# A last stage laid out by expert units, its output product in a bank of its own, and its weights made a stage earlier

## The chip, the cores and the metric

One core of a Trainium2 chip runs the whole program once. The metric is device time in microseconds (us). TensorE (PE), VectorE (DVE), ScalarE (ACT), GpSimd (POOL) and SyncE (SP) each run their own instruction list and meet only at semaphores.

## What is computed

Two transformer-like layers over x of 8 batches x 512 rows x 128 features: attention, a top-2 mixture of experts, a selective scan, and a second mixture of experts. The change is in the last two. In the reference's words, cut:

```python
x = x + ga * L1_attn_ref(h, ...)          # the scan's output added, h = layernorm(x)*(1+ca)+sa
h = layernorm(x) * (1 + cb) + sb
xc = silu(pw_w @ causal_conv3(h) + pw_b); x1 = h + xc
rw = softmax over the top 2 of x1 @ router_w.T + router_b          # 8 experts
ye = silu(x1 @ expert_w + expert_b)       # all 8 experts, 128 -> 128 each
moe = (sum_e rw_e * ye_e) @ out_w.T + out_b
g = norm_w * rms_normalised(x1 + moe)
x = x + gb * (g + gelu(g @ ff_down_w.T + ff_down_b) @ ff_up_w.T + ff_up_b)
```

## The kernel before, in words

The program has five stages, `parts_0` to `parts_d`. After stages 1 to 3 each engine signals an end and waits for all others (`part`, L2503, `end_stage` and `meet`), so no engine is in the last stage, `ffn1` (L2064), before all have left the scan's, `ssm` (L1679). Every engine's order is written out by hand; `Signals` turns names into semaphore waits.

**Scan's stage.** `dve` (L1861) runs a chain of products on T(0)...T(10), [128, 512] each, with ACT giving Exp, Ln and Exp (L1850, L1852, L1854) between them. `low_weights` (L1915, L1918 and L1920) stands in that chain while ACT works. PE then makes eight output products into banks `YB` (L2045 to L2056), DVE adds each to X (L1992), and after the fourth takes the statistics of batch 0 (`dve_bn_group` 0, L1651). Pool turns these into the layer norm's factors (`pool_ln_group`, L1657).

**Last stage.** A batch is 4 tiles of 128 rows. The front of a batch: normalise (`z`, Pool L2121 and ACT L2177), transpose (`zt`, L2392), scale (`hidden`), split into a high and a low part (`hidden` L2195, `low` L2281), convolution product of nine matmuls (`pw`, L2397), `silu`, sum on Pool (`x1`, L2129), split again (`x1h`, `x1l`), router (`route` L2406, `logits`, `best`, `second`, `gates`). Then come the experts: unit u is one tile of 128 rows through all 8 experts (`expert`, L2414, eight matmuls of 512 columns in the bank pair 0-1 or 2-3), ACT's Silu into `ye` (L2219), and DVE's weighted sum `combine(p)` over the pair p of units 2p and 2p+1 (L2333 twice, L2336 fourteen times). Once a batch is summed: `ct` (transposes), `turned`, `out` (L2435, product and x1 added), `bn_out` on DVE (L2339), `rms` on Pool (L2103), `norm` on ACT (L2228, L2233), `hr` (transposes), `fd` (L2450), `gelu` (L2243), `fo` (L2456: per tile one product of the normed rows by DG, L2463, and one of the gelu by FUG, L2464), `final` on DVE (L2345) and the store.

The order of all engines runs over pairs p (L2470 on PE): `front` puts the front of batch p+1 into pair p (0 to 6), so that fronts end at half the experts. `misc` (L2380) deals banks 4 to 7 in turn to every product that is no expert's; a product waits until the one four before it has been read (for `out` that is ACT's `norm`). Pool makes GF, FUG and DG (`last_weights`, L2139: GF is L2163, FUG L2142 and L2146, DG L2150) during pairs 0 to 5, ahead of `rms`.

## Time and profile before

| what | us |
|---|---|
| median of 3 runs | 1002.78 |
| lowest, highest | 998.81, 1006.16 |
| the profiled execution | 1009.28 |
| its span, first to last instruction | 1007.5 |
| PE busy in the span | 840.4 (83%) |
| DVE, ACT, POOL busy | 738.3, 632.3, 496.3 |
| mean granted TensorE clock | 0.909 |

The span is 1.8 us shorter than the time of its own execution. The scan's stage starts near 740 us and ends near 820, the first expert's matmul is at 834.08, the last expert's Silu at 976.15, and the last add ends at 1005.02. A granted clock of 1.00 is 2.4 GHz, one of 0.50 is 1.2 GHz; a 512-column matmul then starts every 0.23 or 0.43 us.

### The profile page before, as it was taken

What the parts mean: (1) busy time and instruction counts of PE and PEld (TensorE: products, weight loads), DVE (VectorE), ACT (ScalarE), POOL (GpSimd) and SP (SyncE); (2) the same over time, 40 slices, a digit from 0 to 9 for tenths busy, and PEclk for the clock granted to TensorE, in tenths of its full rate; (3) what the DMA queues carried; (4) which work ended last, traced back from release to release, by engine and by line L of the source; (5) the groups of instructions that cost most, each with busy time, mean ns of one, the idle gap of its engine ahead of it and who ended that gap; (6) DMA issues with size and microseconds to landing.
All of it is one profiled execution on the core that took longest, in us unless ns stands there. A gap on an engine that the chain in (4) does not pass through costs nothing.

```text
span 1007.5 us, 14225 instructions
## 1 busy us (share of the span) xinstructions
PE 840.4 (83%) x4630; PEld 461.7 (46%) x4630; DVE 738.3 (73%) x1561; ACT 632.3 (63%) x1113; POOL 496.3 (49%) x794
## 2 busy tenths in 40 slices
PE   5689999999988988887796999889946559977986
PEld 4312222222212222221475877777733247766774
DVE  6687878788888778862485888858749577966771
ACT  2157777877766777676484777566715736545562
POOL 3715282727265666355552167656657046653211
PEclk9669999999999999898798999999967878978997
DMA  7735454545536264102115266556360000000000
GB/s 238 153 107 186 91 182 97 166 112 152 125 120 160 107 172 124 68 24 109 52 36 177 97 221 247 195 190 217 115 237 10 24 1 1 0 1 11 22 21 32
DMA packets 45477, 110.78 MB, mean 110 GB/s; under 512 B 7886, under 2 KB 20814, under 8 KB 40086
## 3 DMA queue, kind: packets, MB, share of 16 engines
q1 hardware_dynamic: 39260, 97.93, 32.5%
q0 software_dynamic: 4992, 10.36, 3.0%
q10 hardware_dynamic: 1152, 1.58, 0.5%
q8 instruction: 37, 0.61, 0.3%
q14 instruction: 36, 0.29, 0.1%
HBM read 57.65 MB, written 51.03 MB: 108 GB/s over the span
## 4 chain that ended last, share of the span: by engine, by line
PE 49%; DVE 19%; issue 10%; POOL 10%; ACT 8%; DMA 4%; SPq 0%; another core or an unknown queue 0%; POOLq 0%; DVEq 0%; ACTq 0%
PE PS L1083 10%; DVE mx L891 9%; PE PS L1072 6%; PE PS L1053 4%; PE PS L320 4%; PE PS L322 3%; PE PS L321 3%; POOL yd L1298 3%; DMA HT<-xs 2%; ACT E L798 2%; PE PS L1035 2%; PE PS L1020 1%; ACT ov L804 1%; PE PS L2425 1%; PE PS L2428 1%
## 5 line engine op out<-in xcount | busy, mean ns | idle before, releaser
L891 DVE TENSOR_REDUCE mx<-PS 128x2 f32<-128x1024 f32 x256 | 305.5, 1221 | 76.4 <-PE PS L1053 70.6
L798 ACT ACTIVATE E<-PS 128x512 f32<-128x512 f32 x512 | 277.0, 599 | 85.8 <-PE PS L1072 81.7
L1072 PE MATMUL PS<-Q,K 51*128 51x512 bf16 x512 | 166.0, 396 | 10.6 <-ACT E L798 6.9
L1053 PE MATMUL PS<-K,Q 48*128 48x512 bf16 x512 | 140.6, 409 | 27.1 <-DVE mx L891 26.7
L1083 PE MATMUL PS<-E,V 128*9 128x512 f32 x1024 | 140.1, 620 | 19.5 <-ACT ov L804 18.8
L1298 POOL DMA_INDIRECT yd<-yt,goes x92 | 94.6, 1028 | 49.2 <-DVE yt L1474 25.6
L1072 PEld LDWEIGHTS PS<-Q,K 51*128 51x128 bf16 x512 | 37.0, 95 | 162.1 <-ACT E L798 97.2
L1462 DVE TENSOR_TENSOR Gl<-Gf,Gh 128x512 fp32r<-128x512 f32 x117 | 82.2, 719 | 31.6 <-ACT Gh L1333 22.1
L513 POOL DMA_INDIRECT xs<-HT,pos x64 | 63.8, 996 | 79.5 <-ACT E L798 45.2
L1327 ACT ACTIVATE Gf<-PS,WR 128x512 f32<-128x512 f32 x92 | 63.1, 689 | 48.7 <-PE PS L322 39.3
L2336 DVE SCALAR_TENSOR_TENSOR cb<-ye,gt,cb 128x128 f32<-128x128 f32 x224 | 65.5, 366 | 0.0
L665 POOL CAST mh<-mx 128x32 bf16<-128x32 f32 x16 | 3.4, 211 | 113.1 <-DVE mx L891 113.1
L2219 ACT ACTIVATE ye<-PS 128x1024 f32<-128x1024 f32 x32 | 32.8, 1024 | 37.0 <-PE PS L2428 37.0
L1053 PEld LDWEIGHTS PS<-K,Q 48*128 48x128 bf16 x512 | 29.1, 95 | 58.0 <-DVE mx L891 49.6
L1083 PEld LDWEIGHTS PS<-E,V 128*9 128x9 f32 x1024 | 15.2, 88 | 65.5 <-issue 35.1
L1457 DVE CAST Gh<-Gf 128x512 fp32r<-128x512 f32 x62 | 29.4, 473 | 18.5 <-ACT Gf L1327 17.5
L320 PE MATMUL PS<-Hh,WR 128*128 128x512 f32 x92 | 41.0, 445 | 0.0
L1333 ACT ACTIVATE Gh<-Gf 128x512 fp32r<-128x512 f32 x62 | 39.2, 632 | 2.0
L321 PE MATMUL PS<-Gh,WR 128*128 128x512 f32 x92 | 36.9, 401 | 0.0
L320 PE MATMUL PS<-Gh,WR 128*128 128x512 f32 x92 | 36.8, 400 | 0.0
L322 PE MATMUL PS<-Hl,WR 128*128 128x512 f32 x92 | 36.8, 400 | 0.0
L321 PE MATMUL PS<-Hh,WR 128*128 128x512 f32 x92 | 36.8, 400 | 0.0
(420 smaller groups left out, 1895.1 us busy)
## 6 DMA issues: line engine op xcount, KB each, us to landing
WR<-wsd SPq DMA_DIRECT2D x23, 1028.0 KB
xs<-zero SPq DMA_DIRECT2D x8, 2112.0 KB, 7.4
wsd<-wsp SPq DMA_DIRECT2D x8, 1024.0 KB, 4.1
HT<-xs SPq DMA_DIRECT2D x23, 264.0 KB
dqk<-SPL SPq DMA_DIRECT2D x30, 192.0 KB, 2.8
Q<-dqk SPq DMA_DIRECT2D x14, 384.0 KB
K<-dqk SPq DMA_DIRECT2D x14, 384.0 KB
stage<-in_w SPq DMA_DIRECT2D x9, 516.0 KB
```

The source lines that it names most:

```text
L320: e.matmul(o, wh, xh, start=start, stop=False)
L321: e.matmul(o, wl, xh, start=False, stop=False)
L322: return e.matmul(o, wh, xl, start=False, stop=stop)
L513: e.indirect_dma_start(out=xs[:, :], out_offset=bass.IndirectOffsetOnAxis(ap=pos[:, x, i:i + 1], axis=0), in_=HT[:, i, :], in_offset=None) ...
L798: e.activation(E[:, m % 4, n % 4], PS[:, bank["exp", n], :], ACT.Exp).then_inc(*k.inc("exp", n))
L891: e.tensor_reduce(mx[:, 2 * s % 96:2 * s % 96 + 2], PS[:, o:o + 2, :], AX.X, ALU.max, negate=True).then_inc(*k.inc("max", s))
L1053: return e.matmul(PS[:, o + n % 2, :], Q[r, b % 3, h // 2, qt * P:(qt + 1) * P], K[r, b % 3, h // 2, :], start=True, stop=True)
L1072: e.matmul(PS[:, o, :], K[r, b % 3, h // 2, kt * P:(kt + 1) * P], Q[r, b % 3, h // 2, :], start=True, stop=True).then_inc(*k.inc("exp_mm", n))
L1083: p = e.matmul(PS[32 * j:32 * j + 9, PVB, :], V[:, b % 3, kt, 4 * g + j, :], E[:, m % 4, j, :], start=(kt == 0), stop=(kt == 3))
L1298: e.indirect_dma_start(out=yd[:, :], out_offset=bass.IndirectOffsetOnAxis(ap=goes[:, n % 8, t:t + 1], axis=0), in_=yt[:, n % 2, t * P:(t + ...
L1462: e.tensor_tensor(Gl[:, u % 8], Gf[:, u % 3], Gh[:, u % 8].bitcast(F32), ALU.subtract).then_inc(*k.inc("gl", u))
L2336: m = e.scalar_tensor_tensor(o, y, g, o, ALU.mult, ALU.add)
```

## The change

The end of the scan's stage is no longer a meeting of the engines, and both stages count as one for the semaphores. Pool makes FUG, GF and a new GN (the norm's weight times the gate, per batch) in the scan's stage, after its last `power`; DG goes, and with it PE's product by DG. In its place Pool multiplies the normed rows by GN and adds them to X (`gated`). ACT loads one table set by name before Exp, makes the experts' high part earlier, and touches Silu at the stage's end. DVE makes EWl in the scan's stage, adds batch 0's four tiles on their own with their statistics, then the rest; in the last stage it does `low(0)` before the next statistics, which come in three groups, and x1 of batch 0. PE, ACT and the steps of a batch are ordered by units u with a lag each (`due`). The output product has bank 7 (the last batch's has bank 0) and waits for the `norm` of the batch before; all others share banks 4 to 6, batch 0's first three products use banks 0 to 2. `ct` is due at lag 7, ahead of the `hr` of the batch before; `gelu` precedes the Silu of its unit. On Pool `rms` comes before the same pair's `x1`.

```diff
--- before.py
+++ after.py
...
-        LNG = {0: (0, 4), 1: (4, 12), 2: (12, NT)}
+        LNG = {0: (0, 4), 1: (4, 12), 2: (12, 20), 3: (20, NT)}
...
+                def last_weights():
+
+                    each = lambda n: W[n].unsqueeze(1).to_broadcast([P, 8, P])
+                    k.wait_ge("p3")
+                    k.wait_ge("gb1")
+                    e.tensor_scalar(W["fuT"], W["fuT"], 0.25, None, ALU.mult).then_inc(*k.inc("p"))
+                    e.tensor_tensor(GN[:], GB1[:], each("nwB"), ALU.mult).then_inc(*k.inc("gn"))
+                    k.wait_own("p")
+                    e.tensor_tensor(FUG[:], GB1[:], each("fuT"), ALU.mult).then_inc(*k.inc("fug"))
+                    k.wait_ge("bg1h")
+                    k.wait_ge("bg1l")
+                    e.tensor_tensor(GF, GB1[:], each("fubB"), ALU.mult).then_inc(*k.inc("gf"))
...
                 power(5)
+                last_weights()
                 pool_ln_group(e, k, 0)
...
                 next_weights(4)
+                next_weights(0)
                 out_weights()
+                e.preload_act_table_set("natural_log_exp_and_others")
                 k.wait_ge("zabs")
...
-                next_weights(0)
                 next_weights(2)
                 next_weights(3)
                 k.wait_ge("scan")
                 e.activation(Th[:], T(10), ACT.Copy).then_inc(*k.inc("ch"))
+                e.activation(scr[:, 3:4], half[:, 0:1], ACT.Silu)
...
-                    e.tensor_scalar(cl[:, 0:8], mf[:, 1, 5, :], W["nw"], None, ALU.mult).then_inc(*k.inc("gbn"))
...
+                    k.wait_ge("ewh")
+                    e.tensor_tensor(EWl, W["ewT"], EWh.bitcast(F32), ALU.subtract).then_inc(*k.inc("ewl"))
...
+                for t in range(4):
+                    k.wait_ge("y_mm", t)
+                    e.tensor_tensor(X[:, t, :], X[:, t, :], PS[:, YB[t], 0:P], ALU.add).then_inc(*k.inc("y0"))
+                    k.wait_own("y0")
+                    m = e.bn_stats(stats[:, t, :], X[:, t, :])
+                m.then_inc(*k.inc("bn", "g", 0))
                 for j, (hf, t) in enumerate(YJ):
-                    xv = X[:, 16 * hf + t:16 * hf + 16:4, :]
+                    a = 0 if hf else 1
+                    xv = X[:, 16 * hf + 4 * a + t:16 * hf + 16:4, :]
                     k.wait_ge("y_mm", j)
...
-                    if j == 3:
-                        k.wait_own("ys")
-                        dve_bn_group(e, k, 0)
...
-            DG = stage[:].rearrange("p a n -> p (a n)")[:, 0:1024].rearrange("p (b n) -> p b n", b=8)
...
+            FIRST = {"zd": 0, "pw": 1, "r1": 2}
+            UNITS = 4 * NB
+
+            def due(u, lag):
+
+                b = (u - lag) // 4
+                return (u - lag) % 4 == 0 and 0 <= b < NB, b
...
+                def gated(b):
+
+                    k.wait_ge("hs", b)
+                    k.wait_own("gn")
+                    if b:
+                        k.wait_own("xn")
+                    e.tensor_tensor(hg[:], hs[:, b % 2], GN[:, b:b + 1, :].to_broadcast([P, 4, P]), ALU.mult).then_inc(
+                        *k.inc("hg", b))
+                    k.wait_own("hg")
+                    e.tensor_tensor(xtiles(b), xtiles(b), hg[:], ALU.add).then_inc(*k.inc("xn", b))
 
                 e.memset(Hd[:, :, 0:2], 0.0).then_inc(*k.inc("const", "hd0"))
                 z(0)
                 pool_ln_group(e, k, 1)
                 z(1)
-                x1(0)
-                pool_ln_group(e, k, 2)
-                for p in range(NP + 6):
+                k.wait_own("gf")
+                for p in range(NP + 4):
                     if p + 1 in front:
                         z(front[p + 1])
...
+                        pool_ln_group(e, k, 2)
+                    if p == NP + 2:
+                        rms(NB - 1)
+                    if p % 2 == 0 and 0 <= p // 2 - 3 < NB:
+                        gated(p // 2 - 3)
+                    if p % 2 == 0 and 0 <= p // 2 - 2 < NB - 1:
+                        rms(p // 2 - 2)
                     if p in front:
                         x1(front[p])
...
-                    if 2 <= p < 6:
-                        last_weights(p - 2)
-                    if p % 2 == 0 and 0 <= p // 2 - 2 < NB:
-                        rms(p // 2 - 2)
+                    if p == 2:
+                        pool_ln_group(e, k, 3)
                     if p % 2 and p // 2 < NB:
                         shift(p // 2)
+                gated(NB - 1)
...
                 z(0)
-                e.activation(scr[:, 3:4], half[:, 0:1], ACT.Silu)
                 hidden(0)
                 z(1)
                 silu(0)
                 x1h(0)
...
+                for u in range(UNITS + 10):
+                    p = u // 2
+                    if u % 2 == 0 and p in front:
                         hidden(front[p])
...
+                    for lag, step in ((7, turned), (11, norm), (12, hr), (13, gelu)):
+                        now, b = due(u, lag)
+                        if now:
+                            step(b)
+                    if u < UNITS:
+                        expert(u)
...
                     k.wait_ge("fo_mm", b)
-                    k.wait_ge("xg", b)
+                    k.wait_ge("xn", b)
...
+                k.wait_own("ys")
+                low(0)
                 dve_bn_group(e, k, 1)
-                k.wait_ge("ewh")
-                e.tensor_tensor(EWl, W["ewT"], EWh.bitcast(F32), ALU.subtract).then_inc(*k.inc("ewl"))
-                low(0)
-                dve_bn_group(e, k, 2)
+                k.wait_ge("sx", 0)
+                e.tensor_tensor(X1[:, 0], sx[:, 0], Hd[:, 0, 2:514], ALU.add).then_inc(*k.inc("x1f"))
                 x1l(0)
                 logits(0)
                 best(0)
                 second(0)
-                for p in range(NP + 6):
+                dve_bn_group(e, k, 2)
+                for p in range(NP + 7):
+                    if p % 2 == 0 and 0 <= p // 2 - 4 < NB:
+                        final(p // 2 - 4)
...
+                    if p == 0:
+                        dve_bn_group(e, k, 3)
...
-                    if p % 2 and 0 <= p // 2 - 3 < NB:
-                        final(p // 2 - 3)
...
                 def misc(what, b, *free):
-                    if len(uses) >= 4:
-                        k.wait_ge(*uses[-4])
-                    bank[what, b] = 4 + len(uses) % 4
+                    if b == 0 and what in FIRST:
+                        bank[what, b] = FIRST[what]
+                        return bank[what, b]
+                    if len(uses) >= 3:
+                        k.wait_ge(*uses[-3])
+                    bank[what, b] = 4 + len(uses) % 3
...
                     k.wait_ge("cT", b)
-                    bk = misc("out", b, "hs", b)
+                    if 0 < b < NB - 1:
+                        k.wait_ge("hs", b - 1)
+                    bk = bank["out", b] = 7 if b < NB - 1 else 0
...
-                        e.matmul(o, hT[:, b % 2, t * P:(t + 1) * P], DG[:, b], start=True, stop=False)
-                        m = e.matmul(o, ff[:, b % 2, t * P:(t + 1) * P], FUG[:, b], start=False, stop=True)
+                        m = e.matmul(o, ff[:, b % 2, t * P:(t + 1) * P], FUG[:, b], start=True, stop=True)
...
-                for p in range(NP + 6):
-                    if p in front:
+                for u in range(UNITS + 12):
+                    p = u // 2
+                    if u % 2 == 0 and p in front:
                         zt(front[p])
...
+                    for lag, step in ((8, out), (12, hr), (13, fd), (15, fo), (7, ct)):
+                        now, b = due(u, lag)
+                        if now:
+                            step(b)
+                    if u < UNITS:
+                        expert(u)
+                    if u % 2 == 0 and p - 1 in front:
                         route(front[p - 1])
...
+                    if u % 2 and p in front:
                         pw(front[p])
...
-            if 1 <= st <= 3:
+            if 1 <= st <= 2:
                 end_stage(e, k, st, LAST[i])
                 meet(e, k, st)
...
-            book.stage = max(st, 1)
+            book.stage = min(max(st, 1), 3)
```

## Rows read from the trace of the kernel before

**Rows 1.** Busy time in stretches: expert stage in three parts, one batch, two holes.
```profile
core 0: us, PE busy (x) PEld busy (x) DVE busy (x) ACT busy (x) POOL busy (x), PEclk, DMA share, GB/s
834.08:903.24 69.16, 63.05 (x298) 50.46 (x297) 55.31 (x179) 38.24 (x62) 40.91 (x43) 0.87 0.00 1
903.24:976.15 72.91, 62.09 (x343) 51.56 (x342) 52.40 (x184) 44.22 (x63) 22.26 (x46) 0.95 0.04 15
976.15:1005.02 28.87, 19.95 (x108) 15.56 (x106) 7.92 (x27) 9.32 (x18) 4.73 (x16) 0.83 0.07 28
943.26:957.74 14.48, 13.22 (x76) 10.91 (x76) 10.74 (x38) 9.37 (x14) 3.64 (x9) 1.00 0.05 19
882.67:893.22 10.55, 6.87 (x22) 5.10 (x21) 4.22 (x15) 4.02 (x9) 4.72 (x12) 0.51 0.01 2
904.87:916.88 12.01, 6.24 (x29) 5.54 (x28) 3.81 (x13) 5.21 (x9) 6.74 (x10) 0.72 0.00 1
```

**Rows 2.** Timeline of the two holes (start, length, engine, line, idle before and its releaser).
```profile
879.73 3.32 POOL L2150 TENSOR_SCALAR stage<-p,cl 128x128 f32<-128x128 f32 x4
...
886.52 1.14 ACT L2233 ACTIVATE hs<-PS,lnw 128x128 f32<-128x128 f32 x4 [6.20 <-POOL lnw L2119]
...
887.81 0.77 PE L320 MATMUL PS<-Hdh,PWh 128*128 128x512 f32 x1 [3.68 <-ACT hs L2233]
...
908.10 1.06 PE L2410 MATMUL PS<-p,X 128*128 128x8 f32 x8 [2.83 <-POOL X L2131]
...
912.10 0.77 PE L2463 MATMUL PS<-stage,hT 128*128 128x128 f32 x2 [2.94 <-ACT hs L2233]
```

**Rows 3.** Timeline, one output product in the steady part: its start, the next expert's.
```profile
943.26 0.49 PE L2463 MATMUL PS<-stage,hT 128*128 128x128 f32 x2 [1.26 <-ACT ff L2247]
...
945.06 0.48 PE L2425 MATMUL PS<-rwp,ones 128*128 128x512 f32 x1
```

**Rows 4.** Timeline of VectorE and GpSimd where they meet.
```profile
860.38 2.39 POOL L2142 TENSOR_TENSOR FUG<-GB,p 128x1024 f32<-128x1024 f32 x1
...
860.55 2.27 DVE L2316 TENSOR_TENSOR wk<-wk 128x32 f32<-128x32 f32 x1
...
903.17 3.76 DVE L2336 SCALAR_TENSOR_TENSOR cb<-ye,gt,cb 128x128 f32<-128x128 f32 x14
...
904.20 3.84 POOL L2131 TENSOR_TENSOR X<-sx,Hd 128x512 f32<-128x512 f32 x1 [6.41 <-ACT sx L2202]
...
927.15 4.76 DVE L2336 SCALAR_TENSOR_TENSOR cb<-ye,gt,cb 128x128 f32<-128x128 f32 x14
...
928.38 1.29 POOL L2136 TENSOR_TENSOR X<-X,GA 128x512 f32<-128x512 f32 x1
```

**Rows 5.** Timeline of the scan's chain.
```profile
800.49 1.28 ACT L1852 ACT_TABLE_LOAD   x1
...
800.97 1.22 DVE L1920 TENSOR_TENSOR BGp<-GA,BGp 64x1024 fp32r<-64x1024 f32 x1
...
802.45 0.69 DVE L1966 SCALAR_TENSOR_TENSOR tb<-tb 128x512 f32<-128x512 f32 x1 [0.25 <-ACT tb L1852]
```

**Rows 6.** Timeline of the entry into the last stage.
```profile
820.82 1.65 DVE L1654 BATCH_NORM_STATS2 stats<-X 128x6 f32<-128x128 f32 x8 [0.65 <-POOL scr L2500]
...
821.75 1.28 ACT L2250 ACT_TABLE_LOAD   x1
...
827.77 0.88 ACT L315 ACTIVATE Zd<-X,lnw 128x128 f32<-128x128 f32 x2 [3.20 <-POOL lnw L1677]
...
829.69 0.69 ACT L2202 ACTIVATE sx<-PS,cl 128x512 f32<-128x512 f32 x1 [1.04 <-PE PS L322]
```

**Rows 7.** Timeline of the tail, after the last expert.
```profile
977.61 3.76 DVE L2336 SCALAR_TENSOR_TENSOR cb<-ye,gt,cb 128x128 f32<-128x128 f32 x14
...
986.73 0.60 PE L2389 MATMUL PS<-p,cb 128*128 128x128 f32 x4
...
1000.51 0.80 PE L2463 MATMUL PS<-stage,hT 128*128 128x128 f32 x2 [0.78 <-ACT ff L2247]
...
1004.33 0.69 DVE L2348 TENSOR_TENSOR X<-PS,X 128x512 f32<-128x512 f32 x1 [7.98 <-PE PS L2464]
```

More of the change, by code:

```diff
@@ L1635, in adaln_kernel @@
         GF = GA1[:]
+        FUG = sb("FUG", [P, 8, P])
+        GN = sb("GN", [P, 8, P])
         EWh, EWl = wsp[:, 0:1024], wsp[:, 1024:2048]
@@ L2254, in act @@
                 x1h(0)
[L2255 to L2256 removed]
+                for u in range(UNITS + 10):
+                    p = u // 2
+                    if u % 2 == 0 and p in front:
                         hidden(front[p])
[L2258 to L2278 removed]
+                    for lag, step in ((7, turned), (11, norm), (12, hr), (13, gelu)):
[4 more added lines that the diff above has]
+                        expert(u)
+                    if u % 2 == 0:
+                        if p in CHOICE:
+                            tanh(CHOICE[p])
+                        if p + 1 in front:
+                            z(front[p + 1])
+                        if p - 1 in front:
+                            x1h(front[p - 1])
+                    elif p in front:
+                        silu(front[p])
             def dve(e, k):
@@ L2579 @@
         "owT": I["L1_ffn_out_w"].T, "nw": col(I["L1_ffn_norm_w"]), "fdT": I["L1_ffn_ff_down_w"].T, "fdb": col(np.tile(I["L1_ffn_ff_down_b"], 4)),
-        "fuT": np.tile(I["L1_ffn_ff_up_w"].T, (4, 1)), "fubB": rows(I["L1_ffn_ff_up_b"]),
+        "fuT": np.tile(I["L1_ffn_ff_up_w"].T, (4, 1)), "fubB": rows(I["L1_ffn_ff_up_b"]), "nwB": rows(I["L1_ffn_norm_w"]),
     }
```

84 lines of the change are left out of this document (18 added, 66 removed).

## The prediction

> **What bounds the kernel now.** I read the busy time by stretches first, then the waits, then the timeline around each long one. The change touches only what lies behind 780 us, so I cut that into parts [rows 1]. From the first expert matmul (834.08) to the start of unit 14 (903.24), while fronts run, PE is busy 63.1 of 69.2 us at a clock of 0.87. From there to the last Silu (976.15) it is busy 62.1 of 72.9 at 0.95. The tail takes 28.9 us with PE busy 20.0. PE is the bound of the first two, with holes; the tail is a chain.
>
> In a steady batch of 14.48 us PE works 13.22 and DVE 10.74 [rows 1]; PE's whole idle is 1.26 us ahead of `fo`, which waits for the gelu [rows 3]. So PE bounds it, but DVE is only 2.5 us behind.
>
> Two holes stand out. At 882.67 to 893.22 PE works 6.87 of 10.55 us, at half clock; at 904.87 to 916.88 it works 6.24 of 12.01 at 0.72 [rows 1]. The reader is to see what stands before each [rows 2]: Pool makes half of DG for 3.32 us just when `bn_out(0)` is done, so `rms(0)` is late, ACT stands 6.20 us in front of `norm(0)`, and PE waits 3.68 us with a convolution product whose bank is still `out(0)`'s. In the second, `route(7)` waits 2.83 us for x1 on Pool, and `fo(0)` 2.94 us for the bank that `norm(1)` reads, since `rms(1)` stood behind that x1.
>
> **The change part by part** (sum against the profiled execution: span 1007.5, time 1009.28).
>
> *1. Scan's chain, +2.2.* Three table loads of 1.28 us stand in it [rows 5]. One set for both functions lets Ln follow Exp at once, but DVE's L1966 then waits for DVE itself: L1920 ends at 802.19, L1966 started at 802.45 [rows 5]. So −0.25. On the other side Pool now makes GN and FUG during the last fronts of the scan, 2.39 us each by the same product of 1024 columns [rows 4], and can hold up DVE's `low(5)`, `low(6)` there: 0 to 1.5 us, I take 0.4. GF waits for `bg1l`, that is for L1920, and so starts in the middle of DVE's chain. The nearest row is FUG at 860.38: a DVE instruction with two inputs that began behind it took 2.27 us in place of some 0.2 [rows 4]. Between L1966 and L1968 DVE has a gap for its own semaphore, into which a waiting Pool product can step. 0 to 2.4 us; I take 2.05. EWl moves into DVE's idle time before the transposed inputs land (1.2 us, hidden). Bounds of the part: −0.7 to +3.9.
>
> ScalarE: Activation LUTs of the Trainium skill, section on table sets, says that the set named in the change holds exp and ln both; if it did not, the loads would stay and the −0.25 would be a +1. No row of before can show it.
>
> *2. Entry, +0.3.* The common end (0.65 us from it to the first work) and the Silu load of 1.28 [rows 6] go, and batch 0's statistics come some 1.0 us earlier since four adds of one tile replace one of four tiles. `hidden(0)` started when the load had ended, 823.03; without load, and with all before it 1.1 earlier, it starts at about 821.5. But DVE's statistics of batches 1 and 2 (1.65 us) now stand behind `low(0)`, so their factors come at about 829.4 instead of 827.7, and ACT's order puts `z(1)` (0.88) in front of `silu(0)`: silu starts at 830.4, before at 829.69 [rows 6]. x1 on DVE (0.69 as L1966, against 1.1 on Pool) gives back 0.4. What is late next is `z(1)`. Net +0.3; bounds −2.5 and +1.5.
>
> *3. First stretch (69.2 us), −8.0.* The first hole goes: DG is no longer made here, `rms(0)` follows its statistics, and no convolution product waits for `out`'s bank. That is 3.68 idle plus half of 6.87 busy at 0.51, 3.4, together 7.1 [rows 1, 2]. GF, FUG's two steps and the other half of DG (four blocks of 2.4 to 3.3 us on Pool, by [rows 2, 4]) stop blocking DVE: 1 to 4, I take 1.9. Against it, about 1.0: the statistics of 20 tiles at 0.2 each (1.65 for eight [rows 6]) now stand between DVE's other steps, and the first `gated` comes, on a DVE that is busy 55.3 of 69.2. Bounds −3 to −12: PE's work at full clock is 63.05 less about 6 for the slow part, so 57 is the floor.
>
> *4. Second stretch (72.9 us), −12.8.* Second hole: 5.77 idle and 2.4 by the clock (6.2 busy at 0.72, of which the slow part is from 910 on), 8.2 in all; x1(7) can still be late, so I count 6.5. DG's product: a `fo` takes 1.80 us for eight pairs [rows 3], half of them go: 0.90 × 5 = 4.5. The wait for gelu: 1.26 × 4 = 5.0, since the gelu now stands ahead of its unit's Silu and `fo` comes two experts later. Against it, the two products of `gated` per batch. PE would need 13.22 − 0.90 = 12.32 us a batch. DVE has 10.74, and two more Pool products of 1.1 to 1.3 us (the one at 928.38 [rows 4]) that read SBUF: up to 12.9 to 13.3. I take a period of 13.0, so 0.7 × 4.5 batches = 3.2 back. −6.5 − 4.5 − 5.0 + 3.2 = −12.8. Bounds −16 (nothing held up) and −6.
>
> How long the two hold each other up is the open price. SBUF — State Buffer of the Trainium skill, "Who interferes with whom", says that the first to start has the shared pair for one whole instruction and the other blocks. By that rule a Pool product waits at most one DVE instruction, then takes 1.0 from DVE. The row at 927.15 agrees (the burst grew from 3.76 to 4.76 while `shift` took 1.29), the row at 904.20 doesn't: that Pool sum took 3.84 us, and ended 1.1 us behind a burst that lost nothing [rows 4]. By the page alone the period would be 13.3, by the second row 12.3.
>
> *5. Banks.* A ring of three in place of four: each product waits for one released three uses ago, which are ACT copies or DVE's `logits` and are long done by then. Nothing; if DVE lags by more than 3 us, `fd` waits for `final`, within the bounds above. `out` waits for the `norm` before it: from there to the next `norm` lie out 2.0, combine 4.2, statistics 0.9, rms 2.8, norm 1.1, that is 11 to 12 us in a period of 13. Hidden, with about 1 to spare.
>
> *6. Tail (28.9 us), −7.2.* `combine(15)` ends at 981.37; `ct(7)` waits behind `hr(6)` until 986.73 [rows 7]: 5.4 go. PE is still at full clock then, where now `out(7)` runs at the slow one: −1.7. The last `fo` takes 3.8 us (1000.51 to 1004.33 [rows 7]) and loses half: −1.9. `norm(7)` will stand behind `gelu(6)` on ACT: +0.8. `gated(5)` meets `combine(15)`: +1.0. Sum −7.2; bounds −4 and −10. `gated(7)` (2.4) lies beside hr, fd, gelu, fo (over 5).
>
> Sum: 2.2 + 0.3 − 8.0 − 12.8 − 7.2 = −25.5. The span becomes 982.0, its execution 983.8. This execution was 6.5 above the median of its runs, so I forecast 977.3.
>
> **Rivals.**
> *A. The port pair binds DVE.* DVE's 10.74 plus three Pool products in full, plus lags: 14.1 us a batch, +5 in the second stretch, and +5 in the first, where DVE is busiest. For it: 2.27 us lost to one product. Against: bursts that lost nothing. −15.5: 987.
> *B. PE binds alone.* No lock in the scan (−2.0), period 12.3 (−3.2), first stretch near its floor (−3): −33.7, 969.
> *C. Slower.* The `gated` pair waits for a burst of 3.84 us each, as x1 did, and `rms` of the next batch stands behind it on Pool: 7.7 less the 2.4 of the products = 5.3 late, so `norm`, the single bank of `out`, and PE wait, and the clock falls as in the first hole, 2.8 more. 8.1 for each of six batches: +48.6 on the forecast, 1026. It decides once each batch loses over 4.2 us. Against it: `gated(b)` is released about 7 us before `rms(b+1)` has its statistics.
> *D. It does not do what it says.* The holes move rather than close (ACT's order in pairs 6 and 7, x1 behind `rms`): only fo, the gelu wait and half the tail count, less the scan's loss: −4.5 − 5.0 − 3.6 + 3.2 + 2.5 = −7.4, 995.
>
> **How the numbers follow.** Forecast 0.52, its own range 970 to 984; A 0.22; B 0.14; D 0.08; C 0.04. The range of 963 to 991 takes in A and B with their bounds and leaves out D and C and a little of each edge. A measurement of this kernel tells about 1% (10 us) from no change: faster by more is forecast, A and B, 0.90 with a small part of D; within 1% most of D, 0.06; slower 0.04.
>
> **What would show it.** Right: the stretch of 32 units shortens from 142 to about 121; a steady batch takes about 13.0 us with no PE wait ahead of the FUG products; DVE's burst often reads 4.8 rather than 3.8; no Pool weight work behind the first expert; `ct(7)` directly after the last combine; a DVE instruction of over 2 us in the scan's chain beside Pool's GF; one table load there. Wrong: a batch near 14.5, an ACT wait for Pool's rms of over 3 us in every batch, or PE's clock at 0.5 more than once between the first and the last expert.

## The result, and the profile after

The changed kernel takes 991.77 us (median of 8 runs, 990.16 to 996.03), the kernel before beside it 999.19 (8 runs). The ratio is 0.9922, with an interval of 0.9901 to 0.9943: 7.8 us gained by the ratio, 7.4 between the medians, where the forecast had 25.5. The kernel is faster, but by under 1%, the outcome to which I had given 0.06. 991.8 lies just outside my range of 963 to 991, and nearest to the 995 of rival D.

The profiled run of the changed kernel took 990.16, its span is 988.3. First the stretches, cut as before: first expert to unit 14, then on to the steady part, three batches of it, and the rest (the windows of the kernel after; columns as in [rows 1]).

```profile
core 0: us, PE busy (x) PEld busy (x) DVE busy (x) ACT busy (x) POOL busy (x), PEclk, DMA share, GB/s
828.49:893.24 64.75, 59.57 (x298) 48.70 (x297) 55.63 (x193) 41.16 (x65) 31.81 (x49) 0.95 0.01 1
893.24:914.65 21.41, 18.23 (x97) 15.30 (x96) 19.74 (x64) 11.71 (x18) 10.43 (x20) 0.92 0.04 13
914.65:954.86 40.21, 36.37 (x194) 28.98 (x193) 38.38 (x113) 28.00 (x40) 17.54 (x28) 1.00 0.06 21
954.86:988.30 33.44, 18.11 (x98) 13.22 (x96) 15.20 (x43) 11.40 (x23) 16.01 (x30) 0.86 0.08 31
```

Beside [rows 1]: the first stretch fell from 69.16 to 64.75. PE is no longer the busiest in the steady part: DVE works 38.38 of 40.21, PE 36.37. The batches there are of two kinds in turn. Counted from `bn_out` to `bn_out` they take 12.8 and 14.6 us, in both profiles of this kernel, so two batches take 27.4 and one 13.7 in the mean, where a batch took 14.48. The window of 40.21 holds two short ones and one long. A long one has these two waits in it (PE's `out`, then DVE's weighted sum):

```profile
931.63 0.47 PE L2477 MATMUL PS<-rwp,ones 128*128 128x512 f32 x1 [1.28 <-ACT hs L2264]
...
941.62 0.48 DVE L2358 TENSOR_SCALAR cb<-ye,gt 128x128 f32<-128x128 f32 x2 [1.79 <-ACT ye L2249]
```

The stages, set side by side (us; "scan" is from DVE's first step behind the last transposed input to the copy of the scan's result; "end" is from the start of the last `final` to the span's end). A second profile of each kernel stands beside the first:

```
                      before   before 2   after   after 2   forecast   got, 1st pair   2nd pair
up to the scan chain   798.6     789.1    791.5     793.0        0         -7.1          +3.9
scan                    10.8      10.8     12.5      12.5     +2.2         +1.8          +1.8
entry                   24.7      23.8     24.5      24.9     +0.3         -0.2          +1.0
first expert to u. 14   69.2      67.4     64.8      65.1     -8.0         -4.4          -2.3
unit 14 to last Silu    72.9      72.9     65.5      65.4    -12.8         -7.4          -7.5
last Silu to final      28.2      28.5     22.1      22.0     -7.2         -6.1          -6.5
end                      3.2       3.1      7.5       7.6        0         +4.3          +4.4
```

From the scan chain to the end the first pair of profiles reads 208.9 and 196.8, that is -12.1, and the second 206.5 and 197.4, that is -9.1, against -25.5. The second is nearer to what the medians say. What lies ahead of the scan chain differs by 9.5 us between two executions of the kernel before. Only its last piece belongs to the change: from the issue of the load of `p` to the landing of the last transposed input it is 54.2 us in both profiles of before and 54.9 in both of after. So the part that I called the scan's costs 1.8 and another 0.7, beside my 2.2. No run shows what the 0.7 is.

By the first pair 13.4 us are missing. What they are made of is visible in four places. Two are in the list of PE's waits (behind 820 us of the kernel after; engine, line, what it waited for: total, times, longest):

```profile
engine line waited for: us in total, times, longest us
PE PS L2443 <- POOL X L2163: 5.9, 3, 3.2
PE PS L2443 <- DVE X L2379: 4.0, 1, 4.0
PE PS L2477 <- ACT hs L2264: 3.1, 4, 1.3
PE PS L2493 <- DVE X L2373: 2.8, 3, 1.0
PE PS L2501 <- ACT ff L2278: 2.4, 3, 0.8
PE PS L2420 <- DVE lg L2319: 2.3, 1, 2.3
...
```

L2477 is the first matmul of `out`: it waits for `norm`, since `out` has one bank. L2493 is `fd`, which waits for `final` through the ring of three. Part 5 of the prediction had both at nothing. L2443 is `route`, waiting for Pool's x1. L2420 is `zt`, whose bank of the ring DVE's `logits` had still to read, and part 5 had those "long done by then".

The third place is DVE (its timeline in the steady part, then Pool's):

```profile
922.51 3.75 DVE L2361 SCALAR_TENSOR_TENSOR cb<-ye,gt,cb 128x128 f32<-128x128 f32 x14
926.20 0.87 DVE L2367 BATCH_NORM_STATS2 stats<-PS 128x6 f32<-128x128 f32 x4
...
927.48 6.88 DVE L2361 SCALAR_TENSOR_TENSOR cb<-ye,gt,cb 128x128 f32<-128x128 f32 x14
```

```profile
930.29 1.29 POOL L2168 TENSOR_TENSOR X<-X,GA 128x512 f32<-128x512 f32 x1
931.57 1.30 POOL L2177 TENSOR_TENSOR hg<-hs,GN 128x512 f32<-128x512 f32 x1
932.94 1.27 POOL L2180 TENSOR_TENSOR X<-X,hg 128x512 f32<-128x512 f32 x1
```

`shift` (the sum of X and GA on Pool, L2168) and both products of `gated` run back to back in one burst of combines, and that burst takes 6.88 in place of 3.75: 1.04 for each product. [rows 4] had 1.0 for one. The other burst of the batch loses nothing.

The fourth is the end (Pool's last instruction, then DVE's):

```profile
979.23 1.27 POOL L2180 TENSOR_TENSOR X<-X,hg 128x512 f32<-128x512 f32 x1
```

```profile
980.83 0.69 DVE L2373 TENSOR_TENSOR X<-PS,X 128x512 f32<-128x512 f32 x1 [2.30 <-PE PS L2501]
```

Pool ends at 980.50, the last add starts at 980.83, and the span ends at 988.3. In the kernel before the end comes 3.2 behind the start of that add, and in this one 7.5. The timeline has nothing between. But the view of source line L135, at which the kernel closes, has what each engine's sequencer does there: a DRAIN, with its length in ns and its start in us (the kernel after, then before):

```profile
L135 POOLq DRAIN  x1: 8918/8918/8918, 979.2 to 979.2; - x1
...
L135 DVEq DRAIN  x1: 728/728/728, 980.8 to 980.8; - x1
```

```profile
L135 POOLq DRAIN  x1: 8688/8688/8688, 994.5 to 994.5; - x1
...
L135 DVEq DRAIN  x1: 730/730/730, 1004.3 to 1004.3; - x1
```

Pool's DRAIN runs to 988.1, that is 7.6 us past Pool's last instruction, and the span ends 0.2 later. In the kernel before it also ends 7.6 past Pool's last instruction (995.6), at 1003.2, but that is ahead of the last add and costs nothing.

### The profile page after: what moved, and what is told of

It reads as the page before. It is cut to its first block, busy times and chain, and to the rows that moved or that the text cites. A ratio compares the mean times of both kernels' runs of the same rounds, so it can differ in the third digit from the quotient of the medians.

```text
span 988.3 us, 14132 instructions
## 1 busy us (share of the span) xinstructions
PE 826.2 (84%) x4566; PEld 446.7 (45%) x4566; DVE 756.5 (77%) x1564; ACT 631.0 (64%) x1110; POOL 507.2 (51%) x811
## 4 chain that ended last, share of the span: by engine, by line
PE 38%; DVE 24%; POOL 16%; issue 11%; ACT 7%; DMA 2%; SPq 0%; POOLq 0%; DVEq 0%; ACTq 0%
PE PS L1083 12%; POOL yd L1298 9%; DVE mx L891 8%; PE PS L1072 7%; PE PS L1053 5%; DVE cb L2361 4%; ACT E L798 2%; PE PS L1035 2%; ACT ov L804 1%; PE PS L1020 1%; PE PS L320 1%; PE PS L322 1%; PE PS L321 1%; POOL Gl L1290 1%; PE PS L1040 1%
## 5 line engine op out<-in xcount | busy, mean ns | idle before, releaser
L1298 POOL DMA_INDIRECT yd<-yt,goes x92 | 95.0, 1032 | 44.4 <-issue 22.9
L1462 DVE TENSOR_TENSOR Gl<-Gf,Gh 128x512 fp32r<-128x512 f32 x117 | 86.0, 749 | 22.4 <-ACT Gh L1333 19.1
L1327 ACT ACTIVATE Gf<-PS,WR 128x512 f32<-128x512 f32 x92 | 63.4, 689 | 39.5 <-PE PS L322 38.7
L2361 DVE SCALAR_TENSOR_TENSOR cb<-ye,gt,cb 128x128 f32<-128x128 f32 x224 | 76.0, 412 | 0.0
L2249 ACT ACTIVATE ye<-PS 128x1024 f32<-128x1024 f32 x32 | 32.6, 1026 | 18.0 <-PE PS L2465 14.5
L322 PE MATMUL PS<-Gl,WR 128*128 128x512 f32 x92 | 36.3, 395 | 0.0
L320 PE MATMUL PS<-Gh,WR 128*128 128x512 f32 x92 | 36.3, 394 | 0.0
```

Of the source, the lines that this page charges most:

```text
L320: e.matmul(o, wh, xh, start=start, stop=False)
L322: return e.matmul(o, wh, xl, start=False, stop=stop)
L1298: e.indirect_dma_start(out=yd[:, :], out_offset=bass.IndirectOffsetOnAxis(ap=goes[:, n % 8, t:t + 1], axis=0), in_=yt[:, n % 2, t * P:(t + ...
L1327: e.activation(Gf[:, u % 3], PS[:, u % 3, :], ACT.Gelu_apprx_tanh, bias=w[:, fc:fc + 1]).then_inc(*k.inc("gelu", u))
L1462: e.tensor_tensor(Gl[:, u % 8], Gf[:, u % 3], Gh[:, u % 8].bitcast(F32), ALU.subtract).then_inc(*k.inc("gl", u))
L2361: m = e.scalar_tensor_tensor(o, y, g, o, ALU.mult, ALU.add)
```

## The experiments

Each ratio is to the kernel before, with its interval; "base" is the changed kernel unless said. The five groups of runs, c to g, were compared on one chip each. A stage's length is read from one execution, which need not be a typical one: those of c3 (985.45) and d3 (991.78) were the longest of their runs.

**The same kernel again, and what `gated` costs.**

> The changed kernel unchanged, so that the others have a second profile of it beside them. Its profile had two parts that may be chance: it entered the scan's stage 7.8 us earlier than the kernel before, and 6.4 us lay between its last store's issue and the span's end, against 2.1 before. If both are chance of one execution, this one shows other numbers there and the same 249 us from the scan's first load to the last add. If they belong to the change, they come back. Median 991 to 993.

992.57, 0.992 [0.9887, 0.9953]; span 990.4, all stages from the scan chain on within 0.4 of the first profile, the end 7.6 again. So the 4.3 us of the end belong to the kernel.

```diff
-                    if p % 2 == 0 and 0 <= p // 2 - 3 < NB:
-                        gated(p // 2 - 3)
...
-                gated(NB - 1)
```

> Leaves out the normed rows times GN and their addition to X (gated), so the output lacks that term; nothing takes its place on PE. Theory 1, the port pair: gated's two Pool products lengthen one combine in every batch by about 2.1 to 2.6 us and DVE bounds the steady part; without them a batch falls from 13.7 to about 12.4 us and the whole by 6 to 10 us, to 982 to 986. Theory 2, the layout (bank 7 alone for the output, three banks for the rest, the order by units) costs what the forecast missed: the batch stays above 13.3 us, the whole falls by under 3 us.

This kernel leaves `normed rows x GN` and its addition to X out. 980.32, 0.9808 [0.974, 0.9877]. The end is 3.1, the tail 21.1, the 32 units take 123.5 (base 130.2), and every steady batch takes 12.5 (base 12.8 and 14.6 in turn). Theory 1 holds, with a total below its range of 982 to 986: it left out the end.

```diff
+                    for b in range(NB):
+                        m = e.tensor_scalar(GN[:, b], ident, cl[:, b:b + 1], None, ALU.mult)
...
+                        e.matmul(o, hT[:, b % 2, t * P:(t + 1) * P], GN[:, b], start=True, stop=False)
+                        m = e.matmul(o, ff[:, b % 2, t * P:(t + 1) * P], FUG[:, b], start=False, stop=True)
```

> The changed kernel with the normed rows' product back on PE (a diagonal weight per batch, made by Pool in the scan's stage), and gated gone from Pool. Theory 1: PE then bounds a batch at 13.2 us with DVE at 11, against 13.7 now: 2 to 4 us faster than the changed kernel, 988 to 990. Theory 2: PE gets 0.9 us a batch more and nothing comes back: 4 to 7 us slower than the changed kernel.

981.79, 0.9792 [0.9743, 0.9841]. The product that the change took from PE, back on PE, with its weight made in the scan's stage: 10 us better than on Pool (187.8 from the scan chain to the end, base 196.8). Its windows from unit 14 on (second line the steady part):

```profile
897.80:915.00 17.20, 16.33 (x93) 13.36 (x92) 16.35 (x56) 10.22 (x17) 4.47 (x8) 1.00 0.04 16
915.00:958.60 43.60, 43.60 (x255) 36.36 (x253) 35.62 (x122) 31.98 (x46) 14.67 (x34) 1.00 0.05 19
```

PE is busy in every moment of the steady part, 13.1 a batch. The 0.9 us that `gated` saved on PE is less than it cost: with `gated`, DVE has two stalls of 1.04 more a batch, the Silus of units 14 and 15 lie 9.1 us apart in place of 6.1, and Pool ends late. The gain is more than either theory had.

**The scan's lock.**

```diff
                     k.wait_ge("bg1l")
+                    k.wait_ge("rwp")
                     e.tensor_tensor(GF, GB1[:], each("fubB"), ALU.mult).then_inc(*k.inc("gf"))
```

> GF, Pool's product of 1024 columns, waits until DVE has left the scan's chain. The theory that its hold on the port pair stretched the chain's second step from 0.49 to 2.47 us: the chain from the landing of TP to Th shortens by 2.0 us and the whole by 1.5 to 2.0, to about 990. The rival, that it only moves the wait to Pool's own layer norm chain of batch 0, which follows GF on Pool: the chain shortens and the first expert starts at the same time, 0.

991.17, 0.9904 [0.9872, 0.9937]. The stage shows what the total can't: 10.5 in place of 12.5. The two lines, base (Pool, then DVE):

```profile
795.23 2.80 POOL L1749 TENSOR_TENSOR GA<-GB,p 128x1024 f32<-128x1024 f32 x1 [14.21 <-DVE BGp L1938]
```

```profile
795.12 0.69 DVE L1985 SCALAR_TENSOR_TENSOR tb<-tb 128x512 f32<-128x512 f32 x1
795.85 2.47 DVE L1987 TENSOR_SCALAR tb<-tb,cv 128x512 f32<-128x512 f32 x1
```

and the same DVE instruction of c4, beside which Pool waits:

```profile
797.36 0.49 DVE L1988 TENSOR_SCALAR tb<-tb,cv 128x512 f32<-128x512 f32 x1
```

So 1.98 us for one Pool product. Behind it the entry took 25.6 (base 24.5 and 24.9) and the units 132.1 (base 130.2 and 130.5), and the two us were gone again. Whether they must be is not shown: the last section has how much these stages differ by chance.

**The baseline, Pool's end, the entry, and a first combination.**

> The kernel before, unchanged, for a second profile. Its first profiled execution was 10 us over the median of its runs. If that excess was chance of the stages that the change does not touch, this one lands TP near 790 instead of 798.6, with the same 208.9 us from there to the end of the span; if it was in the last two stages, that stretch is some 4 us shorter here.

999.62, 0.9996 [0.998, 1.0012]; the stages stand in the table above. It is some of both: of the 11.9 us between the two executions 9.5 lie ahead of the scan chain and 2.4 in the last two stages.

```diff
                 def final(b):
+                    if b >= NB - 2:
+                        gated_v(b)
                     k.wait_ge("fo_mm", b)
```

> The changed kernel with the last two batches' gated products on DVE, which is idle in the tail, so that Pool's last work is the rms of batch 7. Between the last add on DVE and the span's end lay 6.8 us in both profiles of the changed kernel, but 2.4 to 2.5 in the kernels whose Pool ended earlier; each time the span ended 7.8 us after Pool's last instruction. Theory: a Pool that works late ends the program 7.8 us later, and that was on the path; now Pool ends some 5 us earlier and the store ends it: 3.5 to 4.5 us faster than the changed kernel, near 988. Rival: the end's length has another cause: no change.

989.04, 0.9894 [0.987, 0.9919]. Pool ends early, the end is 3.2 again, and 2.3 of the 4.3 come back ahead of `final`, where DVE now does two batches of `gated` in the chain. The interval meets the base's, so the total alone doesn't show a gain.

```diff
-                low(0)
                 dve_bn_group(e, k, 1)
+                low(0)
```

> The changed kernel with the statistics of batches 1 and 2 back ahead of low(0) on DVE. Theory: z(1) on ACT stood in front of silu(0) and came late since its factors did; now they are ready 3 us earlier and silu starts when the convolution's product ends: 24.6 us from Th to the first expert become 22.0 to 22.5, the whole 1.5 to 2.5 us faster. Rival: the half clock of PE bounds the way in, and low(0) becomes late: 0.

987.74, 0.9874 [0.9855, 0.9894]. The entry falls from 24.5 to 22.9; the units grow from 130.2 to 133.6 in the profile. The shorter entry is more than chance: it is 21.1 to 23.3 in the five profiles with this order and 24.3 to 25.6 in the eleven that have the old one and no common end. The timed gain of 4 us is larger than the entry's 1.6 and I can't place the rest.

d4 takes c3's product on PE, this order, and a tile of its own for GF, so that it needn't wait for the scan.

> Three repairs together: the normed rows' product on PE, statistics ahead of low(0), and GF in a tile of its own, made before DVE's scan chain. By the single runs: 10.8 us (diagonal product on PE) + 2.0 (GF out of the chain) + 2.3 (entry) under the changed kernel's 992: 976 to 979. If the gains overlap, 980 to 982.

977.73, 0.9764 [0.9742, 0.9786]: 14 us under the changed kernel, 23 under the one before. That lies in the 976 to 979 that were summed from the single runs.

**The bank of `out`.**

```diff
-                    if 0 < b < NB - 1:
-                        k.wait_ge("hs", b - 1)
-                    bk = bank["out", b] = 7 if b < NB - 1 else 0
+                    bk = own("out", b, "hs", b) if b < NB - 1 else 0
```

(`own` gives `out` banks 7 and 6 by turns from batch 3 on, `fo` bank 5, the others bank 4.)

> Base: the changed kernel. From batch 3 on the output product alternates between two PSUM banks, fo has one for itself, and ct, hr and fd share one, so that neither a product of the next batch waits for norm (PE stood 3.1 us in four waits for ACT's hs there) nor fd for final (2.8 us in three). Theory B1 (the single bank closes the loop: out waits for norm, norm for rms, rms for statistics that stand behind the long burst): the steady batch falls from 13.7 to 13.0 to 13.2, the floor that DVE's own busy time of 12.8 leaves, and the second stretch from 65.5 to 62 to 63.5. Theory B2 (DVE with three Pool products in it is the bound, and PE's waits are only its slack): the waits vanish from PE's list and come back as waits for ye's buffers or for cb; the batch stays at 13.6 to 13.7 and the time within 0.5 us.

994.04, 0.9918 [0.9886, 0.9949]. The steady batch (windows of e1, one batch each):

```profile
915.80:928.64 12.84, 12.51 (x69) 10.12 (x68) 12.82 (x38) 9.25 (x14) 4.90 (x6) 1.00 0.05 20
928.64:941.43 12.79, 12.50 (x69) 10.18 (x68) 12.77 (x38) 9.24 (x14) 6.62 (x12) 1.00 0.06 22
```

From batch 4 on every batch takes 12.8, in place of 12.8 and 14.6 in turn (13.7 in the mean), and DVE is busy in all of it: PE's wait for `norm` had been real, and DVE with three Pool products in it binds at 12.8. Theory B1 holds for the batch, by 0.9 us. From unit 15's Silu to the last one it is 52.5, where seven profiles with the base's banks and order there have 54.3 to 54.4. The total didn't move. Some of that is chance: the Silus of units 14 and 15, ahead of what this edit reaches, lie 10.2 us apart in place of 9.1, as PE is at half clock there behind the same wait of 3.2. And the tail is 1.1 longer, with a wait of 2.2 us for `cb` ahead of `ct(7)` (base 0.9).

```diff
+                    if p % 2 == 0 and 3 < p // 2 <= NB:
+                        k.wait_ge("comb", p - 2)
+                        shift(p // 2 - 1)
```

> Base: the changed kernel. From batch 3 on Pool's shift waits for the end of the combine burst in which gated runs, and so falls into the next, short one: bursts of about 5.9 and 4.8 us in place of 6.9 and 3.75. The sum of what DVE loses is the same. B2 (the sum binds): batch stays at 13.6 to 13.7. B1 (the long burst binds, since statistics and rms stand behind it and out's bank waits for them): the batch falls by up to 1 us, to 12.9 to 13.3, about 3 us in all. If a Pool product that comes to a running burst from idle waits for its end, as x1 did, shift loses up to 3.8 us on Pool, the statistics' rms behind it is late, and the batch gets longer than 13.7.

993.5, 0.9898 [0.9859, 0.9937]. The bursts became 5.8 and 3.8, with the third stall in the TENSOR_SCALAR ahead of the long one (0.74 and 0.89 for 0.48). Two batches took 12.5 and 14.0, a mean of 13.3 (base 13.7). From unit 14's Silu to the last it is 63.4 in both, but here 10.7 of it lie between units 14 and 15, ahead of the edit (base 9.1); from unit 15 on it is 52.7, base 54.3. So where in the batch the stalls fall does matter, as B1 had it, by 0.4 us a batch; the total can't show that. In the batch of 14.0 one `gated` product came to a running burst and took 2.81 us for 1.3.

**Pool's end, tested by itself.**

```diff
+                k.wait_ge("ff", NB - 1)
+                e.memset(hg[:, 0, 0:1], 0.0)
```

> Base: the fastest kernel so far (c3's product on PE, batches' statistics ahead of low(0), GF in its own tile; 977.73, last add to end 3.1 us). One memset of one column is added to Pool at its end, behind the last gelu, on a tile that nothing reads. Theory P (the program ends 7.8 us behind Pool's last instruction where nothing else is later): last add to end grows from 3.1 to 6 to 7, the time by 3 to 4 us. Rival (the 4.4 us came from gated itself, from its traffic or from the store of its batch): no change, 977 to 978.

984.56, 0.9811 [0.9763, 0.9859]; span 982.4. The median grew by 6.8, but the intervals of the two kernels meet, and the profile's entry is 2.2 longer by chance (last section); the end shows what the total can't. Pool's last instruction, and the start of the last add:

```profile
974.48 0.10 POOL L2205 MEMSET hg<- 128x1 f32 x1 [5.28 <-ACT ff L2278]
```

```profile
976.56 0.69 DVE L2373 TENSOR_TENSOR X<-PS,X 128x512 f32<-128x512 f32 x1 [4.39 <-PE PS L2503]
```

A memset of 0.10 us that nobody reads ends at 974.58, and the span ends 7.8 us later, as in the changed kernel (980.50 to 988.3). The end grew from 3.1 to 5.8. Theory P holds: a Pool instruction that has nothing to do with `gated` does the same, by the DRAIN behind it, which ends at 982.2.

**The common end.**

```diff
-            if 1 <= st <= 2:
+            if 1 <= st <= 3:
                 end_stage(e, k, st, LAST[i])
```

> Base: the changed kernel, with the common end of all engines behind the scan's stage put back and everything else left. My theory: the common end itself was worth little, since the first work of the last stage hangs on the scan's last product and its statistics either way. Entry 24.5 grows to 25 to 26.5, the time by 0.5 to 2 us. Rival (the common end was a main part of the gain, as engines could run ahead): +3 us or more, entry over 27.5.

996.88, 0.9939 [0.9909, 0.9969]. The entry is 26.3, 1.4 to 1.8 over the base's two profiles and 0.7 over the longest of the eleven with the base's order; the units took 3.2 more in the profile. The total's interval overlaps the base's. So what the common end cost lies between nothing and some 5 us, and I can't narrow that.

**Pool's queue at unit 14.** In the base x1(7) stands behind `rms(1)` (Pool's timeline; the Silu that makes sx(7) ends at 894.2):

```profile
893.64 0.57 POOL L2140 TENSOR_TENSOR lnw<-stats 128x4 f32<-128x4 f32 x1 [4.45 <-DVE stats L2367]
...
897.10 1.28 POOL L2163 TENSOR_TENSOR X<-sx,Hd 128x512 f32<-128x512 f32 x1
```

```diff
+                    if p == 6:
+                        x1(front[p])
                     if p % 2 == 0 and 0 <= p // 2 - 2 < NB - 1:
                         rms(p // 2 - 2)
```

> Base: the changed kernel. In pair 6 Pool's x1(7) comes ahead of rms(1), which waits 4.45 us for its statistics there while sx(7) is ready 2.9 us before x1 starts. Theory Q (Pool's queue order, not the lock, made the 3.2 us wait of route(7) and the half clock behind it, which is the largest single piece of what the second stretch missed): x1(7) starts at its Silu's end, the wait falls under 1 us, units 14 to 15 come 5.5 to 7 us apart in place of 9.1, and the stretch from unit 14 to the last shortens by 2 to 3. Rival (what is saved comes back, since norm(1), now 1.3 us later behind x1, holds out(2) and the combines): route's wait goes and the stretch stays within 0.5 of 65.5.

993.56, 0.9917 [0.9889, 0.9944]. Units 14 and 15 come 4.7 us apart in place of 9.1; 1.8 of the 4.4 are left at the last Silu (61.6 from unit 14's Silu to it, base 63.4), the rest came back as waits for `norm` at `out` (5.7 in four, base 3.1). The span didn't get shorter, since Pool sets its end: Pool's last instruction ends at 980.44 (base 980.50), as the first expert came 0.5 later and Pool's end lies 22.7 behind the last Silu (base 21.8), and the span ends at 988.3 in both. In this profile PE ran at half clock to the end, which put the last add at 984.30 in place of 980.83 and cost nothing: the end shrank from 7.5 to 4.0 (the last `fd` and `fo` of f1, then of the base):

```profile
979.34 2.07 PE L2495 MATMUL PS<-hT,fdn 128*128 128x512 f32 x2 [0.69 <-ACT hT L2274]
982.19 2.08 PE L2503 MATMUL PS<-FUG,ff 128*128 128x128 f32 x8 [0.78 <-ACT ff L2280]
```

```profile
977.73 1.13 PE L2493 MATMUL PS<-hT,fdn 128*128 128x512 f32 x2 [0.69 <-ACT hT L2272]
979.64 1.16 PE L2501 MATMUL PS<-FUG,ff 128*128 128x128 f32 x8 [0.78 <-ACT ff L2278]
```

> Base: f1, with the two banks for out of e1. If the 0.6 us per batch that e1 gave in the steady part is real and was only given back at the passage into it (PE's wait of 2.2 us for cb behind the late x1(7)), both gains stand here: 61 to 63 for the second stretch, 3 to 4 us under the changed kernel. If the gain of either is lost to the other's wait, 64 to 65.5 as before.

991.35, 0.9888 [0.986, 0.9915]. From unit 14's Silu to the last 60.5, base 63.4, f1 61.6: the batches, 14.0 and 13.0 in turn in f1, end up at 12.8. Both gains stand side by side. The wait of 2.2 us that I named stands in e1's tail, though, not at the passage, and here there is one of 2.8 in the tail. In the total the two edits are 3 us at most, inside the intervals.

> Base: the fastest kernel so far (d4), with x1(7) ahead of rms(1). There route(7) waits only 0.9 us, so I expect 0 to 1 us less: 976 to 978, a ratio to the kernel before of 0.975 to 0.977. Rival: rms(1) is later by x1's 1.3 and nothing is gained.

978.42, 0.9758 [0.9733, 0.9784]: the same as d4.

**The first stretch.**

```diff
+                    if p == 2:
+                        pool_ln_group(e, k, 3)
...
                     if p in front:
                         x1(front[p])
-                    if p == 2:
-                        pool_ln_group(e, k, 3)
```

> Base: the changed kernel. The factors of the last 12 tiles (Pool, 5.5 us with a pow of 2.30) come ahead of x1(3), where Pool stands idle 4.66 us, in place of behind it, where ACT's next normalisation waits 5.35 us for them, PE 2.33 us behind that, and the clock is halved for the 3.6 us after. Theory R (this one wait with its clock is what the first stretch missed of its 8.0): the wait for lg goes or falls under 0.5, the stretch from first expert to unit 14 falls from 64.7 to 60.5 to 62. Rival (x1(3), now up to 1.3 us later, takes the wait over, or the next front waits as long): the stretch stays within 1 us of 64.7.

995.86, 0.9927 [0.9903, 0.9952]. In the base ACT and PE stand like this:

```profile
860.00 0.88 ACT L315 ACTIVATE Zd<-X,lnw 128x128 f32<-128x128 f32 x2 [5.35 <-POOL lnw L1679]
```

```profile
862.37 0.79 PE L2420 MATMUL PS<-p,Zd 128*128 128x128 f32 x4 [2.33 <-DVE lg L2319]
```

In g1 both waits are gone, and unit 10's Silu comes 2.4 us earlier, counted from the first. Then:

```profile
876.19 1.88 PE L2443 MATMUL PS<-p,X 128*128 128x8 f32 x8 [3.19 <-POOL X L2163]
```

The next x1 is 3.2 us late, PE falls to half clock behind it, and unit 14 comes 65.2 behind the first Silu, base 63.1. The rival holds. The trace also says why this x1 is late: the Silu that makes its input ends at 871.42, but Pool stands with `rms(0)`, which is ahead of it in the same pair (Pool's timeline of g1):

```profile
871.28 0.58 POOL L2140 TENSOR_TENSOR lnw<-stats 128x4 f32<-128x4 f32 x1 [5.49 <-DVE stats L2367]
...
875.02 1.11 POOL L2163 TENSOR_TENSOR X<-sx,Hd 128x512 f32<-128x512 f32 x1
```

That is the queue of f1 once more, two pairs earlier. f1 turned the two in pair 6 alone; no run turns them in pair 4.

> Base: f3 (gated products on PE, statistics ahead of low(0), GF in its own tile, x1(7) ahead of rms(1)), with the same move of the factors. By theory R 3 to 4 us less than f3: 974 to 975.5, a ratio to the kernel before of 0.970 to 0.973. By the rival 977 to 979.

976.97, 0.975 [0.9714, 0.9787]. d4, f3 and g2 can't be told apart: 977 to 978.4, 23 to 25 us under the kernel before. Nor does g2 show more than f3 by its stages: unit 14 comes 65.0 behind the first Silu, in f3 63.4.

## Why the prediction was wrong

The direction and most mechanisms were right, the size wasn't: 7.8 for 25.5. The steps, in the prediction's order (two measured values are those of the first and the second pair of profiles):

*1. Scan, +2.2:* measured +1.8 in the chain and +0.7 ahead of it. Right in mechanism: one table load stands there, and DVE's L1987 took 2.47 beside GF. c4 shows that the whole of the 1.8 is that product.

*2. Entry, +0.3:* measured -0.2 and +1.0. `z(1)` in front of `silu(0)` is what is late; d3 gives 1.6 back by the order that I had named as the cause.

*3. First stretch, -8.0:* measured -4.4 and -2.3. The first hole closed, as foreseen. What failed is the sum "3.68 idle plus half of 6.87": it took both as gone for good. The stretch is a chain of fronts over four engines, and with the hole gone other waits of it decide: 2.33 us behind Pool's factors with half clock behind (862.8 to 866), 1.7 for x1. The 2.33 ends when DVE's `logits` free a bank, but these stand behind ACT's `x1h`, and that behind the normalisation that waits for the factors. g1 removed this wait, and the next took its place. So the floor of this stretch isn't PE's 57; in every kernel run, with `gated` or without, 63.1 to 65.2 us lie between the Silus of unit 0 and unit 14 (before: 69.6 and 68.4). What sets that floor I haven't settled; x1 behind `rms(0)` in pair 4 is the wait that stands next, and it is untested.

*4. Second stretch, -12.8:* measured -7.4 and -7.5. Two terms failed. First, "I count 6.5" for the second hole: x1(7) was late again, by more than before (3.2 us for 2.8 [rows 2]), since it still stood behind `rms(1)`. f1 shows it. Second, the period: 13.0 forecast, 13.7 measured, and 12.8 once `out` has two banks (e1). At 4.5 batches, as I had counted them, the 0.7 are 3.2 of the 5.4 us missing here, an estimate. My DVE sum, 10.74 plus two Pool products, was right to 0.1: it is the 12.8 of e1. The price of the lock was right too: 3.1 us for three products. "SBUF — State Buffer" of the Trainium skill, in "Who interferes with whom", says that the first to start holds the shared pair for one whole instruction. The products of 1.27 us cost DVE 1.04 each and the one of 2.80 cost 1.98, so trace and page agree there. For Pool's own wait they don't: an x1 that comes from idle at 852.09 takes 2.39 us, and ends 1.5 behind the burst that it met. Which of the two a product meets isn't settled.

*5. Banks, nothing:* wrong. "Hidden, with about 1 to spare" was computed with 4.2 for the combine between two norms. With the lock in it that burst is 6.9, so the spare 1 was gone by my own part 4; I didn't put the two together. `out` waited up to 1.29 a time, `fd` up to 1.0 for `final`. With both undone the batch lost 0.9.

*6. Tail, -7.2:* measured -6.1 and -6.5, right.

*The missing term.* "`gated(7)` lies beside hr, fd, gelu, fo" is true and hid the real cost: that Pool was still at work then. It is 4.3 us. The trace of before had it: Pool's DRAIN of 8.7 us at the kernel's close. Pool was done so early there that it cost nothing, and I never asked when each engine ends, only what stands ahead of the last add.

*The whole.* By the first pair 13.4 us are missing: 4.3 the end, 5.4 the second stretch, 3.6 the first, 1.1 the tail, less 1.0 gained on scan and entry. By the second it is 16.4: 4.4, 5.3, 5.7, 0.7, and 0.3 on scan and entry. The 6.5 us that I took off for the median touch none of this: they move the time forecast, not the gain. But of the profile that I summed against, 2.4 us of waits that the next execution didn't have lay in the very stages of the change.

Of the rivals, D came out nearest in number and partly in kind: the second hole did move rather than close. A named the engine that binds at last, but by 12.8, not 14.1: the 10.74 already had one Pool product in it, and A added three. C didn't happen: no `gated` pair of the changed kernel waited for a burst. Two of my own signs of being wrong came: every other batch took 14.6, near 14.5, and PE was at half clock in three places between the first and the last expert (from 828.5, 862.8 and 901.1). The chances (0.9 for faster by over 1%) stood on signs that were right, the range's upper edge on terms that I had added as if each hole closed alone.

## What to carry to other kernels

When work moves to an engine that runs beside the critical one, add up three bills: what it takes from the engine that shares memory with it, what waits behind it in its own queue, and when that engine now ends. Here the three were 2.1 us of DVE a batch, 3 us once, and 4.3 us at the end, against 0.9 us a batch saved on PE. With only the weight made on Pool, in the scan's stage, and the product left on PE, the kernel was 10 us better (c3). And a buffer that is "just hidden" must be checked with the durations after the change, locks included.

## What the runs showed of the hardware that I had not expected

Pool's DRAIN at the kernel's close ends 7.6 us behind Pool's last instruction in all nineteen profiles, whether that was a product of 1.3 us or a memset of 0.10. DVE's and ACT's take 0.7. In the eleven profiles in which Pool worked late the program's end follows Pool's last instruction by 7.8 to 7.9 (980.50 to 988.3, 982.52 to 990.4, 981.71 to 989.6 among them, and 974.58 to 982.4 with the memset). In the other eight Pool was done 9.3 to 12.1 ahead of the end, and the end comes 3.1 to 3.2 behind the start of the last add. So in this program, as an estimate from these rows, Pool should be done 4.7 us before the last add starts.

TensorE's clock doesn't rise at the same point in the same program. d4 and e3 are the same up to the last gelu. In both PE starts the scan's output at 1.2 GHz after 6.6 us idle, and the first matmul at 2.4 GHz comes 3.5 us behind the start in d4 and 6.4 in e3 (d4, then e3):

```profile
802.74 0.80 PE L2077 MATMUL PS<-WOGh,Th 128*128 128x512 f32 x1 [6.64 <-ACT Th L1878]
...
806.20 0.39 PE L2077 MATMUL PS<-WOGh,Th 128*128 128x512 f32 x1
```

```profile
806.15 0.79 PE L2077 MATMUL PS<-WOGh,Th 128*128 128x512 f32 x1 [6.65 <-ACT Th L1878]
...
812.56 0.40 PE L2074 MATMUL PS<-BGp,ones 128*128 128x512 f32 x1
```

Their entries are 21.1 and 23.3 us, so some 2 us of a stage of one profile are chance, and f1's tail, 26.5 us from the last Silu to the last add where the base has 22.1, was most likely the same. Readings of a single stage under 2 us above stand only where a duration by itself shows them, or where, as with the steady batches, several profiles agree to 0.1.

A DVE instruction with one input tensor (L1987, 2.47 us for 0.49) was held up by a Pool product as much as one with two. The prediction had put the stall at that place, but had only a row with two inputs to price it by [rows 4].
